# Attention probabilities: normalised on GpSimd, multiplied with the values in fp32 for two heads at once, evicted by VectorE alone

## The chip, the cores and the metric

One core of a Trainium2 chip. The metric is the device time of one execution, in microseconds (us). The kernel before takes 1751.86 us, the median of three runs (1751.84 to 1755.15).

## What is computed

Two attention layers and two mixture-of-experts layers on x (2 sequences, 1024 rows, 256 columns), each layer added onto x. Only the attention bears on this change. Both attention layers have 16 heads of 64 columns with **one** key and value head shared by all, a causal mask, an additive bias and a "null" key and value from `cond_64` that every query may also attend to:

```python
...
q = ln(x) @ Wq                     # 16 heads of 64
k, v = split(ln(x) @ Wkv)          # one head of 64, shared
sim = q @ k.T + bias[h]            # layer 0: a table of relative positions; layer 1: the input fside
sim = concat(q @ null_k + null_attn_bias[h], sim)
p = softmax(mask(sim))             # over the null column and the causal keys
out = p @ concat(null_v, v)        # per head
x = x + ln(out @ Wout) * g_out
...
```

## The kernel before, in words

**Slots.** The attention of both layers is one software pipeline of 512 slots n, one slot per head. Sixteen steps T stand one after the other (eight row tiles of 128 query rows, for layer 0 and then for layer 1). A step has 8 units u (4 groups of 4 heads, times 2 sequences), and a unit has 4 slots, k = 0 to 3. In row tile t only t+1 blocks of 128 keys are causal, so a slot works on 1 to 8 blocks; `plan.groups` cuts them into groups of at most four blocks, one PSUM bank `tp` each (768 groups and 2304 blocks in all). Every engine walks through the same slots, with its instructions in an order written out by hand, and engines meet at semaphores only. So within an engine whatever waits holds up all that stands behind it.

**One head, engine by engine.** TensorE (PE) multiplies queries and keys into `sc` (L1198, L1199: two fp16 products per 512 columns, since queries and keys are split into a high and a low fp16 half), three slots ahead of the head's own slot. VectorE (DVE) adds the bias and takes the row's extreme in one custom instruction (L881, `biased`, two slots ahead). ScalarE (ACT) takes the exponential and the row sums (L630, `probs` and `rows`, one slot ahead). In the head's own slot PE transposes `probs`, which are not yet normalised, block by block into `tp` (L1307, fp32). ACT copies `tp` out as fp16 (`p_hi`, L723), DVE subtracts and writes the rest as fp16 (`p_lo`, L965). One slot later PE multiplies (`pv`, helper `three` at L1081 to L1083): three fp16 products per block with the probabilities stationary (128 columns) and the values moving (64 columns), into `op`, with the query rows on the partitions. The bank `tp` comes free for group gi when `p_lo` of group gi-2 is done (L1305).

```python
...
                    last = three(o_h, p_hi[:, gi % 4, cols], p_lo[:, gi % 4, cols], v_hi, v_lo,
                                 j == 0, j == nk - 1)
...
```

**Per unit.** At k = 3 POOL (GpSimd) and ACT work out the null column's weight and the four denominators (`d_null` L506, `p_null` L732, `denom` L511) and POOL the null value's share (`o_null` L514). At k = 1 of the next unit DVE adds it to the product (`o_raw` L860) and takes the reciprocals (`r_den` L863, four columns), and POOL normalises (`o_n` L479). At k = 2 PE transposes the result (L1295, into `sc` or `aux`), ACT and DVE split it into fp16 halves (`ot_hi` L712, `ot_lo` L955), and at k = 0 of the unit after that PE multiplies by Wout (`y`, six products of 256 columns). For later units stand the projection of the queries (k = 1, six products of 256 columns, then ACT's `q_sq` L663 and `q_n` L665, and POOL's `q_r`, `q_n` in layer 0), the transposes of the queries at k = 3 (L1222) with their split by ACT (`q_b` L651, `q_a` L655) and DVE (`q_a` L909), and the product with the null key at k = 0 (L1285, L1286, then `neg_null` L948).

**Loads.** SP's queue loads the bias of four heads at a time into one of two buffers (`load_bias`, L350 to L364). In layer 1 POOL masks the diagonal block of each (L500). POOL also splits the weights of later layers into fp16 halves, one piece at most slots with k = 1 (L449 to L453). Of the execution, the first 87 us set up the pipeline and the last 379 us are the two mixture-of-experts layers.

## Time and profile before

| | |
|---|---|
| runs of the kernel before | 1751.84, 1751.86, 1755.15 us (median 1751.86) |
| the profiled execution | 1753.54 us, of which the span of its instructions is 1751.1 us |
| mean granted TensorE clock | 0.965 of 2.4 GHz |
| busy, of the span | PE 84%, DVE 79%, ACT 71%, POOL 43% |
| attention slots | 87.3 us to about 1374 us |

Busy time counts each instruction from start to end; the next may start before the last has ended. So the distance between the starts of two neighbours that wait for nothing is what an instruction costs its engine, and it is shorter than the duration.

### The profile page before, as it was taken

The numbers are of one execution on the slowest core, as the hardware profiler recorded it, in microseconds if no ns is written. First come the engines' busy times: TensorE is split into PE (matmuls) and PEld (weight loads), VectorE is DVE, ScalarE is ACT, GpSimd is POOL, SyncE is SP. The second block draws the span as 40 slices with busy tenths as digits, with TensorE's granted clock in tenths as the row PEclk, the third lists the DMA queues.
The fourth block names the chain that finished last, engine by engine and source line by source line (L and its number), as shares of the span: only waits on it lengthen the run. The fifth ranks groups of instructions, "written<-read, shape, count | busy, mean of one in ns | idle before, by whom it ended". The sixth has DMA issues, their size and how long they took to land.

```text
span 1751.1 us, 46745 instructions
## 1 busy us (share of the span) xinstructions
PE 1476.3 (84%) x16377; PEld 1085.6 (62%) x16377; DVE 1391.8 (79%) x3587; ACT 1241.2 (71%) x3512; POOL 752.5 (43%) x1412
## 2 busy tenths in 40 slices
PE   2367778787889999987788888999999799999998
PEld 1255556666667777765666666777777555555555
DVE  4556677877888989977788888899999677777777
ACT  1278888888889999987888888889999533233322
POOL 5546676543433434356554332322231366522222
PEclk9668999999999999999999999999999899999999
DMA  4002111211122213111222111222223000000000
GB/s 136 14 16 62 50 61 50 79 62 52 54 74 86 86 63 109 56 38 38 72 64 74 56 67 65 73 79 86 92 98 98 2 25 19 1 1 1 13 13 25
DMA packets 50442, 96.70 MB, mean 55 GB/s; under 512 B 3332, under 2 KB 27028, under 8 KB 50212
## 3 DMA queue, kind: packets, MB, share of 16 engines
q1 hardware_dynamic: 45504, 90.27, 15.8%
q10 hardware_dynamic: 4708, 3.45, 0.7%
q8 instruction: 134, 2.20, 0.5%
q14 instruction: 96, 0.79, 0.1%
HBM read 91.54 MB, written 2.17 MB: 54 GB/s over the span
## 4 chain that ended last, share of the span: by engine, by line
PE 43%; DVE 19%; ACT 17%; issue 10%; POOL 2%; ACTq 0%; DVEq 0%; POOLq 0%
DVE p_lo L965 7%; PE tp L1307 7%; ACT p_hi L723 6%; DVE biased L881 4%; PE sc L1081 3%; PE sc L1082 3%; PE sc L1083 3%; ACT probs L630 3%; PE sc L1198 3%; ACT q_b L651 3%; PE sc L1199 3%; PE op L1081 2%; PE aux L1081 2%; ACT q_sq L663 2%; PE aux L1083 2%
## 5 line engine op out<-in xcount | busy, mean ns | idle before, releaser
L965 DVE TENSOR_TENSOR p_lo<-tp,p_hi 128x512 f16<-128x512 f32 (+3 forms) x768 | 416.3, 554 | 157.0 <-ACT p_hi L723 150.3
L881 DVE CUSTOM_DVE_ANT_0 biased<-sc,bias,neg_null 128x256 f32<-128x256 f32 (+7 forms) x512 | 411.0, 803 | 3.7 <-PE sc L1199 1.4
L1307 PE MATMUL tp<-ident,probs 128*128 128x128 f32 x2304 | 390.9, 279 | 26.5 <-DVE p_lo L965 23.6
L630 ACT ACTIVATE probs<-biased,neg_max 128x256 f32<-128x256 f32 (+7 forms) x512 | 397.9, 777 | 6.9 <-DVE neg_max L881 5.5
L723 ACT ACTIVATE p_hi<-tp 128x512 f16<-128x512 f32 (+3 forms) x768 | 370.2, 495 | 42.7 <-PE tp L1307 32.7
L1081 PE MATMUL op<-v_s,p_hi 128*128 128x64 f16 x2304 | 285.3, 194 | 63.3 <-DVE p_lo L965 46.2
L1307 PEld LDWEIGHTS tp<-ident,probs 128*128 128x128 f32 x2304 | 269.0, 142 | 64.0 <-issue 49.4
L1198 PE MATMUL sc<-k_a,q_a 128*128 128x512 f16 (+3 forms) x768 | 254.8, 332 | 54.0 <-DVE neg_max L881 48.0
L1083 PE MATMUL op<-v_s,p_lo 128*128 128x64 f16 x2304 | 284.3, 194 | 0.0
L1082 PE MATMUL op<-v_s,p_hi 128*128 128x64 f16 x2304 | 284.3, 194 | 0.0
L1081 PEld LDWEIGHTS op<-v_s,p_hi 128*128 128x128 f16 x2304 | 216.3, 99 | 95.2 <-DVE p_lo L965 73.7
L1199 PE MATMUL sc<-k_b,q_b 128*128 128x512 f16 (+3 forms) x768 | 243.0, 330 | 0.0
L1082 PEld LDWEIGHTS op<-v_s,p_hi 128*128 128x128 f16 x2304 | 210.6, 99 | 7.8
L1083 PEld LDWEIGHTS op<-v_s,p_lo 128*128 128x128 f16 x2304 | 210.8, 98 | 0.0
L511 POOL TENSOR_TENSOR denom<-rows,p_null 128x4 f32<-128x4 f32 x128 | 25.7, 201 | 380.7 <-ACT p_null L732 380.7
L570 POOL TENSOR_TENSOR p_lo<-probs,p_hi 128x512 f16<-128x512 f32 x80 | 92.6, 1157 | 214.9 <-ACT p_hi L756 214.5
L756 ACT ACTIVATE p_hi<-probs 128x512 f16<-128x512 f32 x80 | 50.4, 630 | 145.2 <-DVE probs L1063 145.2
L1198 PEld LDWEIGHTS sc<-k_a,q_a 128*128 128x128 f16 x768 | 75.3, 98 | 113.8 <-DVE neg_max L881 72.9
L479 POOL TENSOR_TENSOR o_n<-o_raw,r_den 128x256 f32<-128x256 f32 x128 | 78.6, 614 | 147.0 <-DVE o_raw L860 145.9
L909 DVE TENSOR_TENSOR q_a<-aux,q_b 64x256 f16<-64x256 f32 x256 | 108.2, 423 | 28.5 <-ACT q_b L651 21.0
L1058 DVE SCALAR_TENSOR_TENSOR biased<-sc,biased 128x512 f32<-128x512 f32 x80 | 55.1, 689 | 70.5 <-ACT biased L752 70.5
L752 ACT ACTIVATE biased<-sc 128x512 f32<-128x512 f32 x80 | 47.6, 595 | 87.5 <-PE sc L1083 87.2
(257 smaller groups left out, 3732.3 us busy)
## 6 DMA issues: line engine op xcount, KB each, us to landing
bias<-rel_table SPq DMA_DIRECT2D x4, 2048.0 KB, 8.3
bias<-in_fside_16xSxS SPq DMA_DIRECT2D x4, 2048.0 KB, 8.5
bias<-rel_table SPq DMA_DIRECT2D x4, 1792.0 KB, 8.0
bias<-in_fside_16xSxS SPq DMA_DIRECT2D x4, 1792.0 KB, 7.2
bias<-rel_table SPq DMA_DIRECT2D x4, 1536.0 KB, 7.6
bias<-in_fside_16xSxS SPq DMA_DIRECT2D x4, 1536.0 KB, 6.7
bias<-rel_table SPq DMA_DIRECT2D x4, 1280.0 KB, 5.5
bias<-in_fside_16xSxS SPq DMA_DIRECT2D x4, 1280.0 KB, 6.0
```

The costliest lines, as they stand in the source:

```text
L570: gp.tensor_tensor(h_lo[:, en % 4, :], h_f[:, en % 2, :], h_hi[:, en % 4, :], ALU.subtract)\
L630: ac.activation(probs[:, i % 2, 0:w], biased[:, i % 2, 0:w], ACT.Exp, bias=neg_max[:, u % 2, i % HU:i % HU + 1], scale=-1.0, accum_out=row ...
L723: ac.activation(p_hi[:, gi % 4, 0:nb * P], tp[gi % 2][:, 0:nb * P], ACT.Copy)\
L881: ve.tensor_tensor_reduce(out=biased[:, i % 2, 0:w], in0=sc[i % 2][:, 0:w], in1=bias[:, g % 2, i % HU, 0:w], scale=-1.0, scalar=neg_null[: ...
L909: ve.tensor_tensor(heads(q_a[DH:P, u % 2, :], e), first[e * DH:(e + 1) * DH, 0:UW].rearrange("p (c q) -> p c q", q=P), heads(q_b[0:DH, u % ...
L965: ve.tensor_tensor(p_lo[:, gi % 4, 0:nb * P], tp[gi % 2][:, 0:nb * P], p_hi[:, gi % 4, 0:nb * P], ALU.subtract).then_inc(s["p_lo"], 1)
L1081: te.matmul(out_, l_hi, r_hi, start=first, stop=False)
L1082: te.matmul(out_, l_hi, r_lo, start=False, stop=False)
L1083: return te.matmul(out_, l_lo, r_hi, start=False, stop=last)
L1198: te.matmul(o_, q_a[:, u % 2, cols], k_a[layer][:, bt, c0:c0 + cw], start=True, stop=False)
L1199: last = te.matmul(o_, q_b[:, u % 2, cols], k_b[layer][:, bt, c0:c0 + cw], start=False, stop=True)
L1307: last = te.transpose(tp[gi % 2][:, jj * P:(jj + 1) * P], probs[:, n % 2, (j0 + jj) * P:(j0 + jj + 1) * P], ident[:, :])
```

## The change

- **Normalisation.** The null column becomes one more column of the scores: DVE copies the null score behind the biased scores (`null_col`), ACT's exponential covers w+1 columns, and its row sum is the whole denominator. DVE takes one reciprocal per head. POOL multiplies that head's probabilities by it in place (`scaled`), and the null column's into `pn`. The pipeline gets one slot deeper: scores four slots ahead, `biased` three, `probs` two (in three buffers), reciprocal and scaling one.
- **Product.** Values are kept in fp32 (`v_s`, one copy, 64 columns) and are the stationary operand; the transposed probabilities (`p_t`, fp32, four buffers of a whole head) are the moving one, 128 columns. Two neighbouring heads write to partitions 0 to 63 and 64 to 127 of `op`. One fp32 product per block and head stands for three fp16 products. The pair's product is cut in two parts, in the two slots after the pair. The result comes out transposed.
- **Evictions.** Every group of `tp` is copied to `p_t` by one DVE `tensor_copy`; ACT's `p_hi` and DVE's subtraction are gone. (`plan.copier` could name ACT; it returns 0, DVE, always.)
- **Per unit.** `d_null`, `p_null`, `denom`, `o_null`, `o_raw`, `o_n` and the transposes of the result are gone. ACT and DVE split `op` straight into `ot_hi` and `ot_lo`, now first in slot k = 2. The null value comes in once per step: `pn` is transposed and multiplied with null value times Wout (`nv_w`), one product added to `y`. The transposes of the queries and their split move from k = 3 to k = 2. ACT's four squares with sums become one square and a sum on DVE (`q_ss`, layer 0 only).
- **Loads.** The bias comes for two heads at a time into one of three buffers, and POOL's mask in layer 1 covers two heads.

```diff
+    def copier(self, gi):
+        return 0
...
-        v_s = [sb(f"v_s{i}", [P, B * TILES, 2, DH], F16) for i in range(2)]
+        v_s = [sb(f"v_s{i}", [P, B * TILES, DH]) for i in range(2)]
...
@@ POOL, slot n @@
+                i = n + 1
+                if 0 <= i < N:
+                    pool.wait_ge(s["r_den"], i + 1)
...
+                    gp.tensor_tensor(pn[:, T % 2, bt, hg * HU + i % HU:hg * HU + i % HU + 1], probs[:, i % 3, w:w + 1],
+                                     r_i, ALU.mult).then_inc(s["pn"], 1)
+                    p_i = probs[:, i % 3, 0:w]
+                    gp.tensor_scalar(p_i, p_i, r_i, 1.0, ALU.mult, ALU.mult).then_inc(s["scaled"], 1)
...
@@ ACT, slot n @@
+                if k == 2 and 0 <= m - 1 < NU:
+                    act.wait_ge(s["pv"], 2 * (u + 1))
...
+                    ac.activation(ot_hi[:, :].rearrange("p (c q) -> p c q", q=P), turned(o_t) if u < U0 else o_t,
+                                  ACT.Copy).then_inc(s["ot_hi"], 1)
-                i = n + 1
+                i = n + 2
...
+                    ac.activation(probs[:, i % 3, 0:w + 1], biased[:, i % 2, 0:w + 1], ACT.Exp,
...
-                        for h in range(HU):
-                            ac.activation(q_sq[:, h, :], first[:, h * DH:(h + 1) * DH], ACT.Square,
-                                          accum_out=q_ss[:, h:h + 1]).then_inc(s["q_ss"], 1)
+                        ac.activation(q_sq[:, :, :].rearrange("p h d -> p (h d)"), first[:, 0:UW], ACT.Square)\
+                            .then_inc(s["q_sq"], 1)
...
@@ DVE, slot n, after ot_lo at k == 2 @@
+                i = n + 1
+                if 0 <= i < N:
+                    dve.wait_ge(s["probs"], i + 1)
...
+                    ve.reciprocal(r_den[:, i % HU:i % HU + 1], rows[:, i % HU:i % HU + 1]).then_inc(s["r_den"], 1)
-                i = n + 2
+                i = n + 3
...
+                    ve.tensor_copy(biased[:, i % 2, w:w + 1], null_i).then_inc(s["null_col"], 1)
...
-                        dve.wait_ge(s["p_hi"], gi + 1)
-                        ve.tensor_tensor(p_lo[:, gi % 4, 0:nb * P], tp[gi % 2][:, 0:nb * P],
-                                         p_hi[:, gi % 4, 0:nb * P], ALU.subtract).then_inc(s["p_lo"], 1)
+                            dve.wait_ge(s["pt"], gi + 1)
...
+                            ve.tensor_copy(p_t[:, n % 4, j0 * P:(j0 + nb) * P], tp[gi % 2][:, 0:nb * P])\
+                                .then_inc(s["copy_dve"], 1)
...
@@ PE @@
+            def pv(n0, first_, last_):
...
+                if c == 0 and first_ == 0 and u >= 1:
+                    pe.wait_ge(s["ot_lo"], u)
...
+                for j in range(first_, last_):
+                    for e in range(2):
+                        if j % 4 == 0 or j == first_:
+                            copied(plan.first_group[n0 + e] + j // 4)
+                        last = te.matmul(op[e * DH:(e + 1) * DH, c * P:(c + 1) * P], v_s[layer][:, bt * TILES + j, :],
+                                         p_t[:, (n0 + e) % 4, j * P:(j + 1) * P], start=(j == 0), stop=(j == nk - 1))
+                if last_ == nk:
+                    last.then_inc(s["pv"], 1)
...
+                    part = (n0, 0, (nk + 1) // 2) if n % 2 == 0 else (n0, (nk + 1) // 2, nk)
...
-                        pe.wait_ge(s["probs"], n + 1)
+                        pe.wait_ge(s["scaled"], n + 1)
                         if gi >= 2:
-                            pe.wait_ge(s["p_lo"], gi - 1)
+                            copied(gi - 2)
```

## Rows read from the trace of the kernel before

**Rows 1.** The page: busy time of each engine over the span, us (share) xinstructions

```profile
PE 1476.3 (84%) x16377; PEld 1085.6 (62%) x16377; DVE 1391.8 (79%) x3587; ACT 1241.2 (71%) x3512; POOL 752.5 (43%) x1412
```

**Rows 2.** Stretches: length, each engine's busy time, granted clock, DMA share, GB/s

```profile
87.30:366.30 279.00, 210.72 (x2332) 159.87 (x2332) 195.28 (x637) 230.07 (x907) 171.94 (x342) 0.91 0.17 52
366.30:759.70 393.40, 352.08 (x4632) 272.25 (x4633) 340.73 (x773) 352.85 (x1001) 157.00 (x309) 1.00 0.20 70
759.70:1008.00 248.30, 201.41 (x2426) 156.97 (x2424) 197.21 (x640) 204.91 (x632) 132.41 (x280) 0.97 0.22 61
1008.00:1372.20 364.20, 341.13 (x4551) 267.27 (x4550) 330.99 (x747) 324.92 (x740) 95.97 (x204) 1.00 0.23 79
1276.60:1372.20 95.60, 92.85 (x1270) 73.71 (x1268) 90.84 (x176) 87.50 (x176) 22.50 (x48) 1.00 0.26 89
```

**Rows 3.** The page: shares of the chain that ended last, by engine

```profile
PE 43%; DVE 19%; ACT 17%; issue 10%; POOL 2%; ACTq 0%; DVEq 0%; POOLq 0%
```

**Rows 4.** Groups by line: busy us, mean ns of one, idle before and its releasers

```profile
L965 DVE TENSOR_TENSOR p_lo<-tp,p_hi 128x512 f16<-128x512 f32 (+3 forms) x768 | 416.3, 554 | 157.0 <-ACT p_hi L723 150.3
L723 ACT ACTIVATE p_hi<-tp 128x512 f16<-128x512 f32 (+3 forms) x768 | 370.2, 495 | 42.7 <-PE tp L1307 32.7
L1307 PE MATMUL tp<-ident,probs 128*128 128x128 f32 x2304 | 390.9, 279 | 26.5 <-DVE p_lo L965 23.6 <-ACT probs L630 0.6
```

**Rows 5.** DVE in order of time, eight blocks: start us, us, instruction

```profile
1323.15 0.69 DVE L965 TENSOR_TENSOR p_lo<-tp,p_hi 128x512 f16<-128x512 f32 x1 [0.29 <-ACT p_hi L723]
1323.75 0.41 DVE L860 TENSOR_TENSOR o_raw<-op,o_null 128x256 f32<-128x256 f32 x1
1324.09 0.17 DVE L863 RECIPROCAL r_den<-denom 128x4 f32<-128x4 f32 x1
1324.17 1.25 DVE L881 CUSTOM_DVE_ANT_0 biased<-sc,bias,neg_null 128x1024 f32<-128x1024 f32 x1
...
1325.45 1.51 DVE L965 TENSOR_TENSOR p_lo<-tp,p_hi 128x512 f16<-128x512 f32 x2
```

**Rows 6.** DVE groups, shapes kept apart, columns as in Rows 4

```profile
L965 DVE TENSOR_TENSOR p_lo<-tp,p_hi 128x128 f16<-128x128 f32 x128 | 36.4, 285 | 21.6 <-ACT p_hi L723 20.2
L881 DVE CUSTOM_DVE_ANT_0 biased<-sc,bias,neg_null 128x128 f32<-128x128 f32 x64 | 21.6, 338 | 1.6 <-PE sc L1199 1.4
L909 DVE TENSOR_TENSOR q_a<-aux,q_b 64x256 f16<-64x256 f32 x256 | 108.2, 423 | 28.5 <-ACT q_b L651 21.0
```

**Rows 7.** PE in order of time, eight blocks, first of each run

```profile
1300.50 0.38 PE L1198 MATMUL sc<-k_a,q_a 128*128 128x512 f16 x1
...
1301.37 0.60 PE L1307 MATMUL tp<-ident,probs 128*128 128x128 f32 x4
1301.80 0.19 PE L1081 MATMUL op<-v_s,p_hi 128*128 128x64 f16 x1
...
1302.15 0.41 PE L1295 MATMUL aux<-ident,o_n 128*128 128x128 f32 x2
1302.40 0.60 PE L1307 MATMUL tp<-ident,probs 128*128 128x128 f32 x4
```

**Rows 8.** PE in order of time, one block: six projection products, then the next

```profile
786.89 0.27 PE L1081 MATMUL aux<-wq,xt 128*128 128x256 f16 x1
...
787.54 0.27 PE L1307 MATMUL tp<-ident,probs 128*128 128x128 f32 x1
```

**Rows 9.** Line 1100, the fp32 product: ns min/median/max, first and last start; its stretch

```profile
L1100 PE MATMUL sc<-bias,moe_w x32: 379/379/483, 38.4 to 45.2; 128*128 128x256 f32 x32
...
38.40:45.50 7.10, 7.10 (x33) 6.23 (x34) 1.11 (x4) 0.00 (x0) 6.31 (x14) 1.00 0.00 1
```

**Rows 10.** POOL: a scaling by a column of factors, in order of time; null terms

```profile
171.41 0.48 POOL L451 TENSOR_SCALAR stage<-stage,g_in 128x256 f32<-128x256 f32 x1 [0.28 <-DMA stage<-in_L_cond_Wq]
...
L511 POOL TENSOR_TENSOR denom<-rows,p_null 128x4 f32<-128x4 f32 x128 | 25.7, 201 | 380.7 <-ACT p_null L732 380.7
```

More of the change, by code:

```diff
@@ L69, in __init__ @@
         self.first_group.append(len(self.groups))
+        self.copies = [0, 0]
+        self.copy = []
+        for gi in range(len(self.groups)):
+            e = self.copier(gi)
+            self.copies[e] += 1
+            self.copy.append((e, self.copies[e]))
+    def copier(self, gi):
+        return 0
     def tile(self, n):
@@ L236, in free_banks @@
         def free_banks(n):
-            return 0 <= n < N - 4 and all(plan.tile(i) < TILES // 2 for i in range(n + 1, n + 4))
+            return 0 <= n < N - 5 and all(plan.tile(i) < TILES // 2 for i in range(n + 1, n + 5))
         def banks(n):
@@ L251, in model @@
         setup = sems("setup", """mhalf ident rel kn0 place ones penalty big nss nrinv nkd nt nka nkb
-                    mt cb lg lgh stats rstd z tanh h pt t mm tab""")
-        s = sems("attn", """scores bias biased probs
-                    pt p_hi p_lo pv
-                    q_proj q_ss q_nd q_na q_t q_hi q_lo q_dup q_null null
-                    x_st x_rs xn xt xt_hi xt_lo xr_hi xr_lo kv kv_act kv_r kv_d kv_v k_dup kt k_hi k_lo
-                    d_null p_null denom r_den o_null o_raw o_n ot ot_hi ot_lo y y_s y_acc
+                    mt cb lg lgh nv0 nvs stats rstd z tanh h pt t mm tab""")
+        s = sems("attn", """scores bias biased null_col probs r_den pn scaled
+                    pt copy_dve copy_act pv
+                    q_proj q_sq q_ss q_nd q_na q_t q_hi q_lo q_dup q_null null
+                    x_st x_rs xn xt xt_hi xt_lo xr_hi xr_lo kv kv_act kv_r kv_d k_dup kt k_hi k_lo
+                    pn_t pn_s nv_w nv_o ot_hi ot_lo y y_s y_acc
                     y_st y_rs y_n x_new""")
@@ L265, in model @@
         table_in = sem("table_in")
-        s_bias = [sem(f"bias_in{i}") for i in range(2)]
+        s_bias = [sem(f"bias_in{i}") for i in range(3)]
+        s_copy = [s["copy_dve"], s["copy_act"]]
         s_stage = [sem(f"stage_in{i}") for i in range(2)]
```

335 lines of the change are left out of this document (173 added, 162 removed).

## The prediction, made before any run of the change

> **What bounds the kernel now.** The page first: no engine is full over the whole span, and three of them are busy 71 to 84% of it [rows 1]. So the stages have to be read one by one. In the stretches, a length divided by its slots is the time of one head. Row tiles with 1 to 4 blocks ("small", 128 slots per layer) take 279.0/128 = 2.18 us in layer 0 and 248.3/128 = 1.94 in layer 1; those with 5 to 8 ("large") take 393.4/128 = 3.07 and 364.2/127 = 2.87 [rows 2]. With eight blocks in layer 1, PE is busy 97% of the time, DVE 95% and ACT 92% [rows 2]: three engines share the bound. With one block none is: there the chain decides, and the chain is spread over PE, DVE and ACT [rows 3]. The groups show its weak link. DVE idles 150.3 us before `p_lo` for ACT's `p_hi`, ACT 32.7 us before `p_hi` for PE's transposes [rows 4]: transposes, ACT, DVE, one behind the other, inside each slot. A slot is thus the fullest engine's work plus a slack for that chain.
>
> **DVE's work per slot, by distances between starts.** Bias and extreme: 1.18 + 0.10 us for 1024 columns [rows 5]. `p_lo`: 0.60 for 512 [rows 5], about 0.20 for 128 by its shorter duration (285 against 690 ns) [rows 5, 6], so 0.133 per block + 0.07 per group. Per unit: `o_raw` 0.34, the reciprocal 0.08 [rows 5], `ot_lo` 0.34 like `o_raw` (same 256 columns), two `q_a` of 0.423 [rows 6], 0.15 for the null score; together 1.76, or 0.44 per slot. Statistics and key work of a step I estimate at 0.1 per slot. At the mean large tile (6.5 blocks) that is 1.08 + 1.01 + 0.44 + 0.1 = 2.63 us, at the mean small one (2.5 blocks) 0.55 + 0.40 + 0.44 + 0.1 = 1.49.
> The change takes `o_raw` and its reciprocal from it (0.42 per unit, 0.10 per slot) and adds a reciprocal and a one-column copy in **every** slot: 0.08 each by the reciprocal's distance, at most 0.17 by its duration [rows 5]; I take 0.08, since both stand among other instructions. The copy from `tp` reads as many PSUM columns as `p_lo` did, so it costs the same 0.60 (at best the 0.53 that its columns alone took, at worst `p_lo`'s 0.69 duration). The sum of squares in layer 0 is about `o_raw`'s 256 columns, 0.09 per slot. After: 2.69 large, 1.55 small, +0.09 in layer 0. DVE gets slightly **fuller**: giving it all evictions costs it nothing, because it already passed over every one of them.
>
> **ACT and POOL.** ACT loses `p_hi`, 370 us [rows 4], and is then far from any bound. That is worth nothing by itself; what it gives is the link gone from the chain. POOL's scaling of 256 columns by a column of factors takes 0.48 us [rows 10]; at no more than that per 256 columns, 1024 cost 1.9, plus 0.2 for the null column, by `denom` [rows 10]. POOL was busy 0.26 x 3.09 = 0.7 us of an eight-block slot [rows 2], so 2.5 us at most fit into 3.1. A slot of lead covers the scaling; if POOL's other work (weight pieces) delays it more, PE's transposes wait.
>
> **PE's work per slot.** Scores of 1024 columns 0.87, a transposed block 0.43/4 = 0.108, a block's three fp16 products 0.35/4 = 0.087 [rows 7]. Per unit two six-fold products of 0.65 [rows 8], two pairs of transposes of 0.25 [rows 7], and 0.2 for the eight one-column null products, as an estimate: 2.0, or 0.50 per slot. Large: 6.5 x (0.108 + 0.108 + 0.087) + 0.50 = 2.47; small 1.26. The change takes one pair of transposes (0.06) and swaps 0.087 per block for an fp32 product, whose price I call c. That is **the unknown**. Line 1100's fp32 products appear as two instructions each, 6.8/31 = 0.219 us apart for 256 columns at the full 2.4 GHz clock [rows 9], so 128 columns cost 2 x 0.11 = 0.22 if nothing overlaps. If the two heads' halves of the array work at once, a block costs half, 0.11. No row shows two halves in use, so 0.11 and 0.22 are the ends; I take 0.12, near the lower, since the two heads' outputs lie on separate partitions with separate stationary values. A change between half and whole array could also cost the tail of a product, 0.279 - 0.108 = 0.17 us [rows 4, 7], twice per slot; from 0 to 0.34 I take 0.03. Large: 6.5 x (0.216 + 0.12) + 0.44 + 0.03 = 2.65; small 1.31.
> The Trainium skill bears on this in "TensorEngine Tiling (Array Packing)", § Tiling Modes: tiles work independently, loads and products in parallel, which would put c at its lower end, but a change of the tiling mode drains the array, which would put the second term at its upper end (rival 2). No row here shows either.
> Against the evictions: DVE waited 157 us before `p_lo` in all [rows 4], but it already passed over every group. The Trainium skill, same page, § Performance Considerations, advises both ScalarE and VectorE for PSUM evictions; split so, DVE's large slot would fall from 2.69 to about 2.2 and PE's 2.65 would bound alone. The trace agrees that DVE is near its limit with eight blocks, and differs in that the old sharing, high half by ACT and low half by DVE, relieved DVE of nothing.
>
> **The sum.** Before, the slack over DVE was 3.07 - 2.63 = 0.44 and 0.24 in large tiles (layers 0 and 1), 0.69 and 0.45 in small. An eviction by ACT, 0.5 us on average [rows 4], leaves each slot's chain. Of it I take 0.2 off the small slack, as other waits (reciprocal, scaling, the result's split) come in; off the large slack 0.24 and 0.06, down to 0.20 and 0.18, the least that I allow where PE and DVE are about equal (2.65, 2.69). After: large 2.78 + 0.20 = 2.98 and 2.69 + 0.18 = 2.87; small 1.64 + 0.49 = 2.13 and 1.55 + 0.25 = 1.80. Differences: -0.09, 0.00, -0.05, -0.14 us, times 128: -11.5, 0, -6.4, -17.9, together -36 us. Biases arrive as before (half as much at a time, four to eight slots early); set-up and experts are untouched; the null terms on PE (48 small products twice) I put at +2. The sum is made against the profiled execution, 1753.5 us: less 34 it is 1719.5. The median of the runs is 1.7 below that execution: **1718 us**. Within the tiles the change is uneven: I expect one block to win most (`p_hi` gone), eight to lose some 0.1 to 0.2 us.
>
> **Rivals.**
> 1. *The halves take turns* (c = 0.22), so that the change does not do what its name says. PE then needs 6.5 x 0.436 + 0.47 = 3.30 large, 1.56 small. It alone bounds the large tiles; with 0.12 slack 3.42: +0.35 and +0.55 us, or +45 and +70. Small tiles stay DVE's, 2.16 and 1.84: -3 and -13. With the +2, together +101: **1853 us**. It decides from c = 0.15, where PE's large slot passes the old 2.87. For it: no row shows two halves at work at once. Against: none forbids it.
> 2. *Each change of the array's shape drains it*, the upper end 0.34 per slot. Large 2.96 + 0.12 = 3.08: +0.01 and +0.21, or +1 and +27; small 1.62 on PE, as full as DVE: 2.17 and 1.90, -1 and -5. With the +2, together +24: **1776 us**. Against: from the first of a group's twelve fp16 products to the fp32 transposes after them 0.35 us pass [rows 7], with no gap left for a tail, though that is a change of type and not of shape.
> 3. *Slot k = 2 is overloaded.* `ot_lo` and both `q_a` (1.2 us) now stand in one slot of DVE, behind the whole product of the unit before, while PE's extra work stands at k = 0 (0.85) and k = 1 (0.65). If slots cannot lend each other time, the fuller engine counts slot by slot: large in layer 1 (3.06 + 2.86 + 3.54 + 2.35)/4 = 2.95 in place of 2.87, in layer 0, with the sum of squares, 3.04 in place of 2.98. That is +18 on the forecast: **1736 us**. Against: buffers are two to four deep.
> 4. *Much of the slack goes*: a slot more of depth and ACT free, 0.1 us less in each of 512 slots: **1667 us**. For it: the small tiles' slack is chain.
>
> **Chances.** Forecast 0.42; rival 1 0.27; rival 2 0.13; rival 3 0.11; rival 4 0.07. A measurement of this kernel can tell 0.2%, 3.5 us. Forecast, 3 and 4 make 0.60, of which I give 0.05 away for mixtures with 1 and 2: faster 0.55, same 0.07, slower 0.38. The range reaches from 1670, which takes in the slower half of rival 4, to 1860, which takes in rival 1's centre and a little more; about 0.17 is left out. The fast cases alone would have 1665 to 1750.
>
> **What would show it.** Right: the new product's two-instruction pairs of both heads take 0.22 to 0.25 us per pair of blocks; PE and DVE each above 93% busy with eight blocks, ACT below 60%; no long idle before DVE's copies; slots of one block near 1.65 us in layer 1. Wrong: 0.4 us per pair (rival 1), a gap near 0.17 at each change to and from the product (rival 2), DVE waiting for `ot_hi` or `q_b` at k = 2 with PE waiting for its copies after it (rival 3), or PE waiting for POOL's `scaled`, which no case here prices (POOL's weight pieces in small tiles are the place to look).

## Result and profile after

The change makes the kernel slower: 1952.72 us median (1950.12 to 1955.24, 4 runs) against 1752.77 (1751.84 to 1755.15, 4 runs), a ratio of 1.1138 with a 95% interval of 1.1119 to 1.1158. That is 200 us more than before, 235 us above the forecast and beyond its range.

The page of the kernel after: busy time by engine, the chain that ended last by engine, and the groups by line (busy us, mean ns of one, idle before and its releasers). Line numbers are now those of the changed kernel. `att` is the buffer that holds both the biases and the transposed probabilities `p_t`, so `att<-tp` is the copy into `p_t`. A wait for `neg_max` is a wait for DVE's bias instruction.

```profile
PE 1628.4 (84%) x13961; PEld 1112.4 (57%) x13961; DVE 1434.3 (74%) x4407; ACT 910.3 (47%) x2202; POOL 1017.9 (52%) x1957
PE 22%; DVE 6%; issue 2%; ACT 0%; POOL 0%; DVEq 0%; ACTq 0%; POOLq 0%
L1002 DVE COPY att<-tp 128x512 f32<-128x512 f32 (+3 forms) x768 | 415.5, 554 | 300.5 <-PE tp L1361 294.3
L1361 PE MATMUL tp<-ident,probs 128*128 128x128 f32 x2304 | 408.5, 287 | 135.1 <-POOL probs L507 94.8
L507 POOL TENSOR_SCALAR probs<-probs,r_den 128x256 f32<-128x256 f32 (+7 forms) x512 | 382.8, 748 | 9.1
L1201 PE MATMUL op<-att,v_s 128*64 128x128 f32 x4608 | 366.1, 288 | 20.6 <-DVE ot_lo L896 18.7
L504 POOL TENSOR_TENSOR pn<-probs,r_den 128x1 f32<-128x1 f32 x512 | 97.2, 190 | 470.4 <-DVE r_den L905 468.9
```

Against [rows 1], DVE gained 43 us, ACT lost 331, PE gained 152 and POOL 265. The copy costs 554 ns on average, exactly as `p_lo` did [rows 4], so "the same columns, the same price" held. But DVE now idles 294 us for PE's transposes, and the transposes themselves wait 94.8 us for POOL's scaled probabilities, a wait that did not exist before. The chain list says little here: its shares add up to 30% where they were 91% [rows 3], so the stretches are what to read. Their columns are those of [rows 2], the last row is the tile of eight blocks in layer 1.

```profile
89.30:413.70 324.40, 237.50 (x1971) 158.67 (x1972) 209.92 (x856) 170.87 (x523) 207.37 (x467) 0.86 0.15 44
413.70:857.70 444.00, 393.96 (x3763) 282.20 (x3763) 356.39 (x988) 233.60 (x520) 248.44 (x437) 0.98 0.19 63
857.70:1164.30 306.60, 235.02 (x2088) 162.30 (x2087) 201.59 (x830) 161.97 (x479) 175.44 (x428) 0.90 0.16 48
1164.30:1567.20 402.90, 383.62 (x3690) 275.92 (x3689) 336.61 (x932) 218.60 (x462) 189.26 (x346) 1.00 0.23 71
1459.40:1567.20 107.80, 105.46 (x1013) 76.16 (x1012) 91.19 (x223) 56.09 (x107) 49.95 (x82) 1.00 0.24 77
```

Divided by their slots, one head each, these are:

| us per head | small, layer 0 | large, layer 0 | small, layer 1 | large, layer 1 |
|---|---|---|---|---|
| before [rows 2] | 2.18 | 3.07 | 1.94 | 2.87 |
| forecast | 2.13 | 2.98 | 1.80 | 2.87 |
| after | 2.53 | 3.47 | 2.40 | 3.17 |

The four stretches are 45, 51, 58 and 39 us longer than before: 193 of the 200. The loss is everywhere, so there is more than one cause. The last stretch shows one: with eight blocks PE is 98% busy (105.46 of 107.80) while DVE is at 85% and ACT at 52%. In [rows 2] three engines (PE, DVE, ACT) shared that bound at 97, 95 and 92%. The small tiles show another. Here is the kernel after in order of time at a weight piece in layer 1, with what ended each idle time:

```profile
896.74 0.40 POOL L471 TENSOR_SCALAR stage<-stage 128x256 f32<-128x256 f32 x1 [10.01 <-DMA stage<-in_L_cond_w_up]
897.20 0.40 POOL L474 CAST moe_w<-stage 128x256 f16<-128x256 f32 x1
897.68 0.67 POOL L475 TENSOR_TENSOR moe_w<-stage,moe_w 128x256 f16<-128x256 f32 x1
...
898.47 0.37 POOL L507 TENSOR_SCALAR probs<-probs,r_den 128x128 f32<-128x128 f32 x1
...
898.90 0.48 PE L1361 MATMUL tp<-ident,probs 128*128 128x128 f32 x1 [8.69 <-POOL probs L507]
...
899.41 0.29 DVE L1002 COPY att<-tp 128x128 f32<-128x128 f32 x1 [7.74 <-PE tp L1361]
```

POOL stands 10 us before a weight piece whose load has not landed. The scaling is behind it in POOL's order, the transposes wait for the scaling, the copies for the transposes. POOL waits so seven times, 65.8 us together. Before it waited for loads four times, 3.1 us together. The load is late because of SP's order. SP issues a weight job behind the bias load of pair q = 2L + 3 (L is the job's `load_at`), and by `load_bias` that one waits until 8L + 6 biases are added. In the kernel before, the load stood behind a bias load that waited for 8L. POOL wants the first piece in slot 8L + 1.

### The profile page after: what moved, and what is told of

Its sections match the earlier page's. It is cut to its first block and busy times, and to the rows that moved or that the text cites. A ratio compares the mean times of both kernels' runs of the same rounds, so it can differ in the third digit from the quotient of the medians.

```text
span 1950.2 us, 42760 instructions
## 1 busy us (share of the span) xinstructions
PE 1628.4 (84%) x13961; PEld 1112.4 (57%) x13961; DVE 1434.3 (74%) x4407; ACT 910.3 (47%) x2202; POOL 1017.9 (52%) x1957
## 3 DMA queue, kind: packets, MB, share of 16 engines
HBM read 91.51 MB, written 2.17 MB: 48 GB/s over the span
## 5 line engine op out<-in xcount | busy, mean ns | idle before, releaser
L1002 DVE COPY att<-tp 128x512 f32<-128x512 f32 (+3 forms) x768 | 415.5, 554 | 300.5 <-PE tp L1361 294.3
L654 ACT ACTIVATE probs<-biased,neg_max 128x257 f32<-128x257 f32 (+7 forms) x512 | 397.5, 776 | 435.7 <-PE tp L1361 224.7
L1361 PE MATMUL tp<-ident,probs 128*128 128x128 f32 x2304 | 408.5, 287 | 135.1 <-POOL probs L507 94.8
L922 DVE CUSTOM_DVE_ANT_0 biased<-sc,att,neg_null 128x256 f32<-128x256 f32 (+7 forms) x512 | 410.3, 801 | 11.8 <-ACT probs L654 6.7
L507 POOL TENSOR_SCALAR probs<-probs,r_den 128x256 f32<-128x256 f32 (+7 forms) x512 | 382.8, 748 | 9.1
L1201 PE MATMUL op<-att,v_s 128*64 128x128 f32 x4608 | 366.1, 288 | 20.6 <-DVE ot_lo L896 18.7
L504 POOL TENSOR_TENSOR pn<-probs,r_den 128x1 f32<-128x1 f32 x512 | 97.2, 190 | 470.4 <-DVE r_den L905 468.9
L1201 PEld LDWEIGHTS op<-att,v_s 128*64 128x64 f32 x4608 | 245.7, 138 | 87.5 <-DVE ot_lo L896 39.4
L1084 DVE SCALAR_TENSOR_TENSOR x<-tp,comb,x 128x256 f32<-128x256 f32 x256 | 105.7, 474 | 0.0
L675 ACT ACTIVATE q_b<-aux 64x256 f16<-64x256 f32 x256 | 95.3, 372 | 6.7 <-PE aux L1264 3.4
L654 ACT ACTIVATION_READ_ACCUMULATOR probs<-biased,neg_max 128x1 f32 x512 | 96.3, 188 | 0.0
```

The lines of the kernel that those rows point to most:

```text
L504: gp.tensor_tensor(pn[:, T % 2, bt, hg * HU + i % HU:hg * HU + i % HU + 1], probs[:, i % 3, w:w + 1], r_i, ALU.mult).then_inc(s["pn"], 1)
L507: gp.tensor_scalar(p_i, p_i, r_i, 1.0, ALU.mult, ALU.mult).then_inc(s["scaled"], 1)
L654: ac.activation(probs[:, i % 3, 0:w + 1], biased[:, i % 2, 0:w + 1], ACT.Exp, bias=neg_max[:, u % 2, i % HU:i % HU + 1], scale=-1.0, accum ...
L922: ve.tensor_tensor_reduce(out=biased[:, i % 2, 0:w], in0=sc[i % 2][:, 0:w], in1=bias[:, q % 3, i % 2, 0:w], scale=-1.0, scalar=null_i, op0 ...
L1002: ve.tensor_copy(p_t[:, n % 4, j0 * P:(j0 + nb) * P], tp[gi % 2][:, 0:nb * P])\
L1084: ve.scalar_tensor_tensor(x_t, tp[i // 2][:, (i % 2) * D:(i % 2 + 1) * D], weight, x_t, ALU.mult, ALU.add).then_inc(f["y"], 1)
```

## The experiments

Theory A, at the start: the small tiles lose to POOL's order (loads, then pieces), the large ones to PE. The rivals were DVE's evictions, the overloaded slot k = 2, and a chain of waits as such. The eight-block slots of layer 1 quoted below are the last row tile's stretch over its 31 distances. Every run's ratio is against the kernel before on the same chip.

### Weight loads earlier

```diff
-                if n_jobs < 10 and q == 2 * load_at(n_jobs) + 3:
+                if n_jobs < 10 and q == 2 * load_at(n_jobs) + 2:
```

> The changed kernel with one number altered: SP's queue issues each weight load one bias load earlier (q == 2*load_at + 2 instead of + 3), so that it waits for the same head's scores, biased(8L), as in the kernel before; in the changed kernel it waits for biased(8L + 6), which comes after POOL has already reached the first piece of that load. Theory A (POOL stands still seven times for a weight load, 65.8 us in all, and now holds PE's transposes behind it, PE idle 59.8 us): 1953 falls by 50 to 70 us, to 1885 to 1900, and no POOL wait on a load above 4 us is left. Rival B (the loads land in time that PE lacks anyway, PE is the bound): less than 15 us. Rival C (DVE's evictions bound): less than 15 us.

Measured 1892.41 us, ratio 1.0788 (1.0756 to 1.0820): 60 us back from one digit, and POOL waits for no load any more. The transposes' group and the stretches of this run:

```profile
L1361 PE MATMUL tp<-ident,probs 128*128 128x128 f32 x2304 | 406.5, 286 | 73.6 <-DVE att L1002 40.0 <-POOL probs L507 32.6
85.80:394.40 308.60, 244.24 (x1971) 162.73 (x1971) 209.74 (x856) 170.57 (x523) 207.41 (x467) 0.86 0.15 46
394.40:825.50 431.10, 391.91 (x3763) 280.69 (x3764) 356.33 (x988) 233.64 (x520) 248.45 (x437) 1.00 0.20 65
825.50:1103.30 277.80, 228.81 (x2088) 158.54 (x2087) 201.25 (x829) 161.62 (x479) 175.54 (x428) 0.95 0.18 53
1103.30:1506.30 403.00, 383.66 (x3691) 275.89 (x3691) 336.77 (x933) 218.61 (x462) 189.31 (x346) 1.00 0.23 71
```

The wait for POOL fell from 94.8 to 32.6 us. The large tiles of layer 1 did not move (402.9 to 403.0): their cause is another. Layer 1's small stretch won 29 us, and its granted clock rose from 0.90 to 0.95, with PE's idle time down from 72 to 49 us.

### Three others on the kernel after

Half of the evictions to ACT:

```diff
-        return 0
+        return gi % 2
```

> The changed kernel with copier returning gi % 2: every other group of transposed probabilities is evicted by ACT (busy 47%) instead of DVE. Theory A (PE's product and switches bound the large tiles, POOL's scaling the small ones): less than 25 us gained, large tiles of layer 1 stay above 3.0 us per slot. Rival C (all evictions on DVE are what costs): DVE loses half of 415 us, and the time falls by 80 us or more. Rival D (ACT now blocks on the transposes and delays its exponentials): up to 30 us slower.

Measured 1962.60 us, ratio 1.1188 (1.1156 to 1.1221). The last tile's stretch:

```profile
1463.80:1573.30 109.50, 105.11 (x1014) 75.87 (x1010) 73.91 (x190) 68.49 (x137) 50.00 (x82) 1.00 0.24 77
```

DVE falls from 85 to 68% and eight blocks get slower, 3.53 us in place of 3.48; 10 us are lost in all. DVE's evictions were not the bound.

The queries' transposes and splits back to slot k = 3, as before:

```diff
-                if k == 2 and 0 <= m + 2 < NU:
+                if k == 3 and 0 <= m + 2 < NU:
```

(at its three places, on PE, ACT and DVE)

> The changed kernel with the queries' transposes and their split by ACT and DVE moved back from slot k = 2 to k = 3. Rival K (slot k = 2 holds ot_lo, both q_a and the sum of squares of DVE behind the product's end): 15 to 40 us faster. Theory A: within 10 us, since DVE waits for PE and not the other way (DVE idle 294 us before its copies for PE's transposes).

Measured 1966.67 us, ratio 1.1212 (1.1161 to 1.1262): 14 us slower, by which theory A's 10 us are missed too. PE's scores in this run:

```profile
L1235 PE MATMUL sc<-k_a,q_a 128*128 128x512 f16 (+3 forms) x768 | 257.9, 336 | 99.8 <-DVE q_a L956 45.4 <-ACT q_a L679 42.2 <-issue 9.7
```

They wait 88 us for the split of the queries, for which they wait 2.0 us with the split at k = 2: at k = 3 it is late for scores four slots ahead. So the move brings a wait of its own, and does not test slot k = 2 alone. The large tiles won 6 and 2 us in spite of it, the small ones lost 8 and 13. The gain of 15 to 40 us that the prediction's rival 3 would have in this move did not come; a small part of it in the large tiles is not ruled out.

The scaling on ACT in place of POOL, for i = n + 1, behind the exponential of the slot (and DVE's reciprocal also waits for POOL's `pn` of four heads before):

```diff
-                    p_i = probs[:, i % 3, 0:w]
-                    gp.tensor_scalar(p_i, p_i, r_i, 1.0, ALU.mult, ALU.mult).then_inc(s["scaled"], 1)
...
+                    act.wait_ge(s["r_den"], i + 1)
+                    ac.activation(probs[:, i % 3, 0:w], probs[:, i % 3, 0:w], ACT.Copy,
+                                  scale=r_den[:, i % HU:i % HU + 1]).then_inc(s["scaled"], 1)
...
+                        dve.wait_ge(s["pn"], i - HU + 1)
```

> The changed kernel with the scaling of the probabilities (w columns) on ACT instead of POOL; POOL keeps the one-column product pn, the weight pieces and the rest. Theory A with POOL's part: both the seven waits for loads (60 us of PE) and the short waits of small tiles (PE idle about 2.2 us at a time for POOL) go, the time falls by 80 to 120 us, small tiles of layer 1 come to 1.9 us per slot or less; large tiles change by less than 0.1 us per slot. Rival B (PE's work alone makes the loss): less than 20 us. Rival E (ACT's work in its own queue, 1.0 us of scaling at eight blocks, holds its exponentials up): slower in the large tiles by 0.2 us per slot.

Measured 2055.54 us, ratio 1.1718 (1.1673 to 1.1764): 103 us slower, where theory A expected a gain. The groups on ACT (line 652 is the exponential, line 659 the scaling):

```profile
L652 ACT ACTIVATE probs<-biased,neg_max 128x257 f32<-128x257 f32 (+7 forms) x512 | 396.4, 774 | 217.6 <-issue 116.1 <-PE tp L1366 56.4 <-POOL pn L504 41.1
L659 ACT ACTIVATE probs<-probs,r_den 128x256 f32<-128x256 f32 (+7 forms) x512 | 393.1, 768 | 97.2 <-DVE r_den L910 95.5
```

ACT now waits 95.5 us for DVE's reciprocal inside its own queue, and the next exponential is behind that wait and behind the scaling itself. The large tiles got 0.31 us (layer 0) and 0.38 us (layer 1) a slot slower, 88 us together, with ACT at 71 and 72%: this is rival E, and more than its 0.2. The small tiles of layer 1, where theory A expected its gain, got 20 us slower. POOL waits for loads as before. How much of it is the wait and how much the added work in ACT's order, this run does not part. The lesson: moving a waiting step to an engine with time to spare puts the wait ahead of what is queued there.

### What holds the small tiles

All that follows has the earlier loads in it. The weight pieces from slots k = 1 to k = 2:

```diff
-                if k == 1 and job_end[2] <= split[0] < job_end[9] and n >= 2 * HU * load_at(pieces[split[0]][0]):
+                if k == 2 and job_end[2] <= split[0] < job_end[9] and n >= 2 * HU * load_at(pieces[split[0]][0]):
```

> On top of the kernel with the earlier weight loads (1892 us, slots of 1.98 to 2.37 us in the small tiles of layer 1). POOL's weight pieces move from the slots k = 1 to the slots k = 2. Theory A (in small tiles the scaling is late because POOL, which takes its work in order, has a wait for DVE's y statistics and then a piece of three instructions, 1.5 to 2 us, in the same slot k = 1 ahead of the next scaling): the 67 us in which PE waits for POOL's scaled probabilities fall by half or more, small tiles win 0.05 to 0.2 us a slot, 1860 to 1880 us; tiles of 5 to 8 blocks stay (3.48 us at 8 blocks in layer 1). Rival B (small tiles are held by the chain scores, bias, exponential, reciprocal, scaling, transposes itself, wherever the piece stands): 1887 to 1897 us.

Measured 1883.68 us, ratio 1.0744 (1.0720 to 1.0767): 9 us, between A and B, and the interval still touches that of the run before (1.0756 to 1.0820). The transposes' group of this run:

```profile
L1361 PE MATMUL tp<-ident,probs 128*128 128x128 f32 x2304 | 404.6, 285 | 57.3 <-DVE att L1002 39.9 <-POOL probs L507 16.4
```

The wait for POOL halves again, to 16.4 us, but the time falls by little: POOL is late, and then something else is nearly as late. PE's scores wait 75.7 us for the bias now, where they waited 60.3.

POOL scales one column only:

```diff
-                    gp.tensor_scalar(p_i, p_i, r_i, 1.0, ALU.mult, ALU.mult).then_inc(s["scaled"], 1)
+                    gp.tensor_scalar(p_i[:, 0:1], p_i[:, 0:1], r_i, 1.0, ALU.mult, ALU.mult).then_inc(s["scaled"], 1)
```

> On top of the kernel with the earlier weight loads. POOL scales one column of the probabilities in place of all of them (what is left out: the normalisation of the keys' probabilities, so the attention output is not divided by the denominator); every wait stays. It takes 0.11 us per slot off POOL at one block and 0.85 at eight. Theory A (POOL's length matters in the small tiles, where POOL is 54 to 74% busy and late): small tiles win 0.05 to 0.25 us a slot, 1850 to 1880 us in all, large tiles within 0.03 of 3.48. Rival B (POOL is late for its waits and not for its work): no more than 5 us of gain. Rival C (POOL is a hidden bound in the large tiles too): 8 blocks fall under 3.40 us a slot, 1840 us or less.

Measured 1880.70 us, ratio 1.0715 (1.0680 to 1.0751), at the slow edge of A. Eight blocks stay at 3.48. One column still costs 0.27 us, so 245 of the scaling's 383 us are gone, and they are worth 12 us: its length is nearly hidden, its order was not.

The product of a pair of heads in one slot:

```diff
-                    part = (n0, 0, (nk + 1) // 2) if n % 2 == 0 else (n0, (nk + 1) // 2, nk)
+                    part = (n0, 0, nk) if n % 2 == 0 else (n0, nk, nk)
```

> On top of the kernel with the earlier weight loads. The product of a pair of heads runs in one slot in place of two halves: the same instructions with half the changes between the whole array and its column halves. Each pair of changes costs 0.19 us by the trace (transposes to product 203 ns against 109, product to transposes 202 against 109). Theory A (PE is the bound in tiles of 5 to 8 blocks, 87 to 98% busy, and the changes are part of it): 0.1 us a slot there, 25 us, and some of it in small tiles: 1850 to 1875 us. Rival B (PE is not the bound, or uneven slots cost what the changes give back): 1885 to 1900 us or more.

Measured 1884.44 us, ratio 1.0746 (1.0730 to 1.0762): 8 us, the edge of B, and again an interval that touches that of the earlier loads. Eight blocks went from 3.48 to 3.43 us. Half of the changes of shape gave less than A said, and less than half of the 0.30 us a slot that is found for them below. The trace shows where the rest went: in the slots without a product PE now stands before its scores.

```profile
1445.36 1.04 PE L1361 MATMUL tp<-ident,probs 128*128 128x128 f32 x8
1446.84 0.38 PE L1235 MATMUL sc<-k_a,q_a 128*128 128x512 f16 x1 [0.44 <-DVE neg_max L922]
```

In the last tile such waits for the bias are 4.9 us, where there were none, and over the run they grow from 60.3 to 111.0 us. The uneven slots gave much of the gain back.

With that, and with the pieces at k = 2, the output's evictions one slot earlier and behind the slot's other work:

```diff
-                if k == 2 and 0 <= m - 1 < NU:
+                if k == 1 and 0 <= m - 1 < NU:
                     u = m - 1
                     act.wait_ge(s["pv"], 2 * (u + 1))
```

(ACT's `ot_hi` now stands behind the exponential, DVE's `ot_lo` behind the bias)

> On top of the kernel with earlier weight loads and the pieces at k = 2 (1884 us): the product of a pair in one slot, and with it the two evictions of the unit's output (ACT ot_hi, DVE ot_lo) at k = 1 behind the exponential and the bias of that slot, in place of k = 2 ahead of the reciprocal and the bias. Theory A (in tiles of 1 to 4 blocks PE is held by the outputs' single bank: DVE begins slot k = 2 with ot_lo, which waits for ACT's ot_hi, which waits for the product that PE has just ended; the bias behind it comes late, and with it the scores; 13 to 19 us of PE's weight loads wait for ot_lo and 30 us of its scores for the bias in the small tiles of layer 1): these waits fall by half, small tiles win 0.05 to 0.15 us a slot, large ones 0.04 as with the product in one slot alone: 1845 to 1870 us. Rival B (the waits move to the next one in the chain, or ot_lo at k = 1 delays DVE's copies as much): 1872 to 1890 us.

Measured 1850.96 us, ratio 1.0554 (1.0536 to 1.0572): 33 us under the run with the pieces moved. The product in one slot had given 8 alone, so the evictions' place is worth some 25, if the two add up. The total is in A's range, the place is not: the large tiles won 11.5 and 9.2 us, the small ones 10.1 and 2.3. Product and scores of this run:

```profile
L1201 PE MATMUL op<-att,v_s 128*64 128x128 f32 x4608 | 314.1, 281 | 0.0
L1235 PE MATMUL sc<-k_a,q_a 128*128 128x512 f16 (+3 forms) x768 | 254.5, 331 | 136.1 <-DVE neg_max L915 133.2 <-DVE q_a L956 2.0
```

PE's wait for `ot_lo` (18.7 us after the change, 28.5 with the product in one slot) is gone. The scores now wait 133 us for the bias, where they waited 75.7 in the run with the pieces moved. Most of that growth is not the evictions': the product in one slot alone had taken this wait from 60.3 to 111.0.

DVE's split of the queries behind the copies of its slot (the six lines from `dve.wait_ge(s["q_hi"], ...)` moved down, otherwise as the last run):

```diff
-                if k == 2 and 0 <= m + 2 < NU:
-                    u = m + 2
-                    dve.wait_ge(s["q_hi"], 2 * (u + 1))
...
                 now = plan.at(n)
...
+                if k == 2 and 0 <= m + 2 < NU:
+                    u = m + 2
+                    dve.wait_ge(s["q_hi"], 2 * (u + 1))
```

> On top of the kernel with loads, pieces, one slot per product and output evictions at k = 1 (1851 us). DVE's two splits of the queries (q_a, 0.88 us, behind a wait for ACT) stand behind the copies of slot k = 2 in place of ahead of them. Theory A (what is left in tiles of 1 to 4 blocks is DVE late with the bias, for which PE's scores wait 44 us in the small tiles of layer 1; the split of the queries, for which DVE waits 16 us, is a cause of it: the copies behind it come late, and PE's scores two slots on): 1830 to 1846 us, small tiles 0.03 to 0.15 us a slot faster. Rival B (the bias of the next slot is as late behind the split as the copies were): within 5 us of 1851. Rival C (the queries are late for their own scores then): slower, 1856 us or more.

Measured 1901.13 us, ratio 1.0858 (1.0838 to 1.0878): 50 us slower, the number of rival C, but not its mechanism: the scores wait only 2.0 us for the queries' split, and 195 us for the bias (133 before). Nor is it in the small tiles, which A was about and which stay within 4 us; the large ones lose 21 and 25 us. Why is open. What keeps the small tiles 38 us above the kernel before after all edits (295.7 + 269.7 us against 279.0 + 248.3) was not found.

### What holds the large tiles

PE in order of time in the run with pieces at k = 2, eight blocks, first of each run:

```profile
1450.75 0.60 PE L1361 MATMUL tp<-ident,probs 128*128 128x128 f32 x4
1451.28 1.09 PE L1201 MATMUL op<-att,v_s 128*64 128x128 f32 x16
1452.30 0.66 PE L1361 MATMUL tp<-ident,probs 128*128 128x128 f32 x4
1452.79 0.38 PE L1235 MATMUL sc<-k_a,q_a 128*128 128x512 f16 x1
```

Eight transposes and eight block-and-head products take 2.04 us. Each transpose needs 0.108 [rows 7]. In the middle of the 16 product instructions the starts are 0.006 and 0.103 us apart in turn, so a block and head costs 0.109. That makes 16 x 0.109 = 1.74, and leaves 0.30 us a slot for going to column halves and back: 0.09 more before the first product, 0.05 more to the second, 0.10 more before the first transpose after them and 0.055 to the one behind it. Two runs test these two readings, and a third takes the product's price down. In order, head by head, on top of the pieces at k = 2:

```diff
-                for j in range(first_, last_):
-                    for e in range(2):
+                for e in range(2):
+                    for j in range(first_, last_):
```

> On top of the kernel with earlier weight loads and the pieces at k = 2 (1884 us): within a half product the blocks of the first head all stand ahead of those of the second, so that neighbouring instructions use the same column half, not the other one. Theory A (the halves work side by side only when neighbours in the queue are on different halves; the fp32 product costs 0.129 us per block and head so, and about 0.22 when they take turns): 0.09 us more per block and head, 0.7 us a slot at 8 blocks, 2010 to 2090 us in all. Rival B (0.129 us is what one half takes by itself, and nothing overlaps): no change, 1878 to 1890 us.

Measured 1936.29 us, ratio 1.1044 (1.1022 to 1.1066). Eight blocks take 3.85 us, 0.37 more than 3.48: between A and B. The same 16 instructions in this run:

```profile
1448.98 1.58 PE L1201 MATMUL op<-att,v_s 128*64 128x128 f32 x16
1450.49 0.66 PE L1361 MATMUL tp<-ident,probs 128*128 128x128 f32 x4
```

They take 1.51 us against 1.02. So the halves do work side by side, and the order head, other head, head is what lets them; in order, the starts are 0.11 us apart at both ends of the group, and only in its middle, where one head's blocks meet the other's, are they closer.

The whole array and no change of shape (the product left out, the identity in its place):

```diff
-                        last = te.matmul(op[e * DH:(e + 1) * DH, c * P:(c + 1) * P], v_s[layer][:, bt * TILES + j, :],
-                                         p_t[:, (n0 + e) % 4, j * P:(j + 1) * P], start=(j == 0), stop=(j == nk - 1))
+                        last = te.matmul(op[:, c * P:(c + 1) * P], ident[:, :],
+                                         p_t[:, (n0 + e) % 4, j * P:(j + 1) * P], start=(j == 0 and e == 0), stop=(j == nk - 1 and e == 1))
```

> On top of the kernel with earlier weight loads and the pieces at k = 2 (1884 us). What is left out: the product uses the identity as its stationary values, on the whole array and for both heads into the same 128 columns, in place of the values on one column half for each head; so no change of the array's shape is left, and nothing can work side by side. Theory A (by the trace a block and head costs 0.109 us with both halves at work, and the two changes of shape per slot 0.30 us: at 8 blocks transposes and product take 2.04 us where 16 x 0.109 make 1.74): the product doubles to 0.218 us and 0.30 goes, so 8 blocks in layer 1 cost 0.57 us more, 4.0 to 4.1 us, 5 blocks 0.1 to 0.25 more, 1960 to 1990 us in all. Rival B (the changes cost 0.03 us a slot, as the prediction took, and the rest is waits): 8 blocks 0.8 us more, 4.3 us or above, 2030 us or more in all.

Measured 1970.53 us, ratio 1.1241 (1.1182 to 1.1299). PE in order of time, and the last tile's stretch:

```profile
1491.68 2.03 PE L1201 MATMUL op<-att,ident 128*128 128x128 f32 x16
1493.54 0.60 PE L1361 MATMUL tp<-ident,probs 128*128 128x128 f32 x4
1493.98 0.38 PE L1235 MATMUL sc<-k_a,q_a 128*128 128x512 f16 x1
...
1461.90:1585.80 123.90, 123.38 (x1013) 105.27 (x1011) 91.86 (x223) 56.02 (x107) 49.95 (x82) 1.00 0.21 64
```

Eight blocks take 4.00 us, 0.52 more than 3.48, with PE full (123.38 of 123.90). The product's own price rose by 8 x 0.109 = 0.87, so the missing changes gave back about 0.35. Some 0.06 of that is not theirs: PE stood 2.3 us in the last tile's stretch before (107.90 less 105.55, the pieces at k = 2), and stands 0.5 now. That leaves 0.30, as by the starts. The four transposes behind the product show half of it directly: from their start to the scores' 0.44 us pass here and 0.49 with the halves, and from those before the product 0.44 against 0.53. Theory A stands: going to column halves and back costs 0.30 us per slot.

The product in fp16, on the kernel with earlier loads:

```diff
+        p_h = att[:, 6 * S:10 * S].bitcast(F16).rearrange("p (a n) -> p a n", a=4)
...
-        v_s = [sb(f"v_s{i}", [P, B * TILES, DH]) for i in range(2)]
+        v_s = [sb(f"v_s{i}", [P, B * TILES, DH], F16) for i in range(2)]
```

(the copies write `p_h` and the product reads it; probabilities and values are rounded to fp16 so)

> On top of the kernel with the earlier weight loads. The transposed probabilities and the values are rounded to fp16, so the product is one fp16 pass per block and head in place of an fp32 product (0.129 us per block and head by the trace); the placing in column halves, the copies and all waits stay. Theory A (PE's work is the bound in large tiles): a block and head costs 0.05 to 0.07 us, 0.06 less; at 8 blocks 0.5 us a slot less PE work, so DVE (2.95 us of work at 8 blocks) is next: 8 blocks at 3.0 to 3.1 us in layer 1, 1770 to 1820 us in all. Rival B (a chain of waits is the bound): 1860 us or more. Rival C (the changes of the array's shape and the weight loads set the price, not the passes): the product falls by under 0.03 us per block and head, 1850 us or more.

Measured 1841.62 us, ratio 1.0501 (1.0483 to 1.0518): 51 us, between A and C. The last tile's stretch, and the product in order of time:

```profile
1364.10:1461.20 97.10, 87.23 (x773) 57.42 (x770) 90.70 (x222) 56.14 (x107) 49.95 (x82) 1.00 0.25 86
1405.51 0.41 PE L1202 MATMUL op<-att,v_s 128*64 128x128 f16 x8
1405.85 0.66 PE L1362 MATMUL tp<-ident,probs 128*128 128x128 f32 x4
```

The product takes 0.34 us in place of 1.02, 0.085 less per block and head, but the slot only went from 3.48 to 3.13: DVE is at 93% then. One bound was standing just behind the other. In the small tiles nothing was won: they took 5 and 9 us more than with the earlier loads alone, at granted clocks of 0.78 and 0.84 in place of 0.86 and 0.95.

The edits that gained, together (earlier loads, pieces at k = 2, the product in one slot with the output's evictions at k = 1, fp16), and of every second head the second group evicted on ACT:

```diff
-        return 0
+        return int(self.groups[gi][1] > 0 and self.groups[gi][0] % 2 == 1)
```

> The four edits together: earlier loads, pieces at k = 2, the product in one slot with the output's evictions at k = 1, the fp16 product, and of every second head the second group of blocks evicted on ACT instead of DVE. With the fp16 product alone DVE was 93% and PE 90% busy at 8 blocks (3.14 us a slot in layer 1). Theory A (with the fp32 passes gone PE's load falls under DVE's, so that now moving 0.34 us of copies per slot to ACT helps, which in the kernel with the fp32 product it did not): 8 blocks in layer 1 at 2.85 to 3.0 us, under the 3.09 of the kernel before, and 1770 to 1800 us in all. Rival B (ACT's order costs what DVE wins, as with half of the evictions on ACT before): 8 blocks at 3.1 us or more, 1815 us or more.

Measured 1787.18 us, ratio 1.0191 (1.0168 to 1.0213), in A's range; eight blocks take 3.02 us, just above the 3.00 that A allowed and under rival B's 3.1. Its four stretches:

```profile
89.30:385.60 296.30, 212.66 (x1678) 144.59 (x1679) 208.50 (x856) 170.63 (x524) 208.39 (x469) 0.84 0.16 50
385.60:771.80 386.20, 316.47 (x2955) 220.66 (x2953) 329.06 (x926) 246.59 (x582) 247.20 (x435) 0.99 0.22 71
771.80:1038.20 266.40, 199.82 (x1745) 142.78 (x1744) 198.27 (x827) 162.80 (x482) 174.85 (x428) 0.90 0.18 55
1038.20:1398.50 360.30, 306.76 (x2880) 213.90 (x2877) 309.96 (x871) 231.22 (x524) 189.33 (x346) 1.00 0.23 79
```

The large tiles are now 7.2 and 3.9 us **shorter** than in [rows 2]; what is left of the loss in the tiles is in the small ones, 17.3 and 18.1 us, and their granted clock is lower than before (0.84 and 0.90 against 0.91 and 0.97); no run parts that clock from the waits. With PE's load down, evictions on ACT stand in a kernel that gains, though this run does not price them alone. No version beat the kernel before.

## Why the prediction was wrong

**Where the 235 us above the forecast are.** From the table: 0.40 x 128 = 52 and 0.60 x 128 = 76 in the small tiles, 0.49 x 128 = 63 and 0.30 x 127 = 38 in the large ones, and 6 outside the tiles. By cause: 60 are the weight loads, shown by a run. The dear tail of a change of shape, shown by a run too, makes at most 58 by the prediction's own sum (its rival 2, at 0.34 us a slot, against its forecast). The other 117, half of the miss, no run puts down to one step. Edits of order (the pieces, the product in one slot, the output's evictions) gave back 41 us, a part of which is the tail's, since the product in one slot halves the changes. What the rest is, is open.

**"Biases arrive as before."** This step failed first, and cost 60 us (1952.72 to 1892.41), shown by a run that changes only it. The biases did arrive. What I did not count is the other thing in SP's order: a weight load behind a bias load. With the biases cut in pairs, the bias load ahead of it was one whose wait came 6 biases later. The forecast's own last line named the place (PE waiting for POOL's `scaled`, weight pieces in small tiles) but gave it no price and no chance; it was only the half of the reason that lies on POOL. Every load behind a changed wait has to be followed through its queue.

**"A slot of lead covers the scaling."** Right on its length: the run with one column gained 12 us, and 1024 columns took 1.12 us, not up to 1.9. (The POOL share of the eight-block row in that step is 22.50/95.60 = 0.24; the 0.26 stands in its DMA column. The 0.7 us made of it is right.) Wrong on its order: with the piece in the same slot, PE still waited 32.6 us for it after the loads were mended, and 16.4 after the pieces were moved.

**The tail of a change of shape, 0.03 us taken between 0 and 0.34.** It is 0.30, near the upper end. The argument against rival 2 took a change of type, fp16 products to fp32 transposes, as the nearest row; it said itself that this was not a change of shape. The sentence from the Trainium skill, "TensorEngine Tiling (Array Packing)", § Tiling Modes (a change of the tiling mode drains the array), spoke against the change. The trace agrees in that each of the two changes costs about 0.15 us; that draining is what takes them, no run here shows. At 6.5 blocks PE's work is, by the prediction's form, 6.5 x (0.216 + 0.109) + 0.44 + 0.30 = 2.85 us, not 2.65. That moves the bound from DVE to PE. DVE's own work held: 2.69 forecast and 336.61/127 = 2.65 us busy in layer 1, 2.78 forecast and 356.39/128 = 2.78 in layer 0.

**c = 0.12.** Right: 0.109, with neighbours on different halves. Rival 1 did not happen, although the time came out as if it had, and beyond it. A time near a rival's number is no evidence for the rival.

**The slack.** The forecast let 0.18 to 0.20 us stay over DVE in large tiles and took 0.2 off in small ones because ACT's eviction left the chain. In large tiles of layer 1 the slot is 3.17, 0.32 over PE's 2.85. In small tiles of layer 1 the slack over DVE did not fall from 0.45 to 0.25, it grew, to 0.62 even with the loads mended (277.8/128 = 2.17 less 1.55): the chain lost one eviction and got a reciprocal, POOL's scaling, a wait for the output's single bank and the query split in a slot of its own. The run with the output's evictions moved shows how little of that is one wait: it won 12 us in the small tiles. That ACT's hop would be worth 0.2 us a slot was never priced by a row, and no run found it.

**What was right.** DVE's evictions cost what `p_lo` did and are not the bound; ACT is below 60%; PE is above 93% with eight blocks. Of its other signs of being right three failed: DVE is at 85% with eight blocks, not above 93%; one block takes 2.38 us a slot in layer 1 (857.7 to 933.9 us, 32 slots), not 1.65; and DVE idles 294 us before its copies. Of its signs of being wrong two came: a gap at each change to and from the product (0.15 us, it said near 0.17, rival 2), and PE waiting for POOL's `scaled`. Rival 2 had its mechanism right, with a chance of 0.13, and not its time, 1776 us.

## What to carry to other kernels

When a wait on an in-order queue changes, list what is issued behind it on that same queue and price the latest of it: here a weight load behind a bias load cost 60 us, and no engine's busy time shows that. When a change adds a new shape of tiles on TensorE, count the changes per slot and take the dear end of the range until a trace shows the cheap one, and batch the work of one shape only where the slots stay even. A step whose length fits into its new engine's idle time can still be late in order; ask what stands ahead of it.

## What the runs showed of the hardware

- A change of TensorE's array from whole to column halves and back costs 0.30 us by the starts, and as much by taking it away, more than the product of two fp32 blocks (0.22).
- Two column halves overlapped in fp32 as far as neighbouring instructions alternated between them: 16 instructions in 1.02 us alternating and 1.51 in order.
- The granted clock was lower where PE stood more: 0.97 in the small tiles of layer 1 before [rows 2], 0.90 after, 0.95 with the loads mended, 0.84 with the fp16 product. The work of those tiles was the same in the second and the third.
- GpSimd's scaling of 256 fp32 columns by a column of factors took 0.48 us, as [rows 10] had it, but 1024 columns took 1.12 and not four times as much, and one column took 0.27. The group in the run with the pieces moved, eight blocks:

```profile
L507 POOL TENSOR_SCALAR probs<-probs,r_den 128x1024 f32<-128x1024 f32 x29 | 32.6, 1124 | 0.2
```
